# Moving a projection, two score products and a reciprocal within an attention tile of a fused four-layer kernel

## The reference

```python
x = x + tanh(g_xattn[0]) * attention(layernorm(x), mask, ctx, Wq, Wk, Wv, Wo, gate)
x = x + tanh(g_ffn[0])   * top1_experts(layernorm(x), wg, W, b)
x = x + tanh(g_xattn[1]) * wkv(w, u, k=layernorm(x), v=ctx)
x = x + tanh(g_ffn[1])   * top2_experts(layernorm(x), w_gate, w1, w2, w3)
```

## Time and profile before

| | us |
|---|---|
| median of 3 runs | 498.11 |
| range of the runs | 497.46 to 499.47 |
| the profiled execution, its own time | 498.84 |
| its span in the trace | 496.7 |
| PE busy in the span | 461.7 (93%) |
| DVE busy | 376.7 (76%) |
| ACT busy | 259.4 (52%) |
| POOL busy | 175.8 (35%) |

### The profile page before, as it was taken

One profiled execution on the slowest core, in us unless ns is written; L12 is line 12 of the kernel. 1 busy time (PEld: TensorE's weight loads), 2 busy tenths in 40 slices (PEclk: granted clock), 3 DMA queues, 4 the chain that ended last, 5 costly groups with the idle time before them and its releaser, 6 DMA issues. The chain is left out here.

```text
span 496.7 us, 10389 instructions
## 1 busy us (share of the span) xinstructions
PE 461.7 (93%) x3123; PEld 347.1 (70%) x3124; DVE 376.7 (76%) x1007; ACT 259.4 (52%) x562; POOL 175.8 (35%) x228
## 2 busy tenths in 40 slices
PE   4979999998999999999989999999999999999993
PEld 2648677686686776866857755566777878788782
DVE  5876788998988889989877889767867566566540
ACT  2765384572752845737513343326565766657641
POOL 4134213225124232241131160315446557555522
PEclk9999999999999999999999899999999999999998
DMA  7951304004022040040130689648566767768511
GB/s 217 287 107 29 63 1 86 18 13 86 22 44 53 21 84 15 12 84 16 38 69 21 255 341 366 193 116 298 170 205 215 251 183 245 223 197 252 162 22 21
DMA packets 24769, 63.37 MB, mean 128 GB/s; under 512 B 5176, under 2 KB 15296, under 8 KB 21792
## 3 DMA queue, kind: packets, MB, share of 16 engines
q1 hardware_dynamic: 19456, 56.38, 37.2%
q0 software_dynamic: 4416, 6.03, 6.6%
q10 hardware_dynamic: 864, 0.54, 0.3%
HBM read 48.79 MB, written 5.24 MB: 109 GB/s over the span
## 5 line engine op out<-in xcount | busy, mean ns | idle before, releaser
L2021 PE MATMUL bank_o<-w,hT 128*128 (+1 forms) x276 | 68.3, 389 | 1.9 <-issue 1.0
L1406 DVE TENSOR_TENSOR wl<-lw,wh 128x1024 fp32r<-128x1024 f32 (+1 forms) x54 | 60.9, 1129 | 1.1 <-ACT wh L639 1.1
L2021 PEld LDWEIGHTS bank_o<-w,hT 128*128 128x128 f32 (+1 forms) x276 | 48.8, 189 | 16.2 <-issue 11.4
L639 ACT ACTIVATE wh<-lw 128x1024 fp32r<-128x1024 f32 (+1 forms) x54 | 52.9, 981 | 1.8 <-DMA lw<-in_w 1.8
L1091 DVE TENSOR_REDUCE mx<-bank_s 128x8 f32<-128x512 f32 x64 | 42.6, 687 | 11.0 <-PE bank_s L1756 10.7
L498 POOL TENSOR_SCALAR rstd<-mv 128x1 f32<-128x1 f32 x32 | 9.3, 289 | 111.5 <-DVE mv L1011 111.5
L1754 PE MATMUL bank_s<-Kh,Qx 128*128 128x128 f32 x256 | 40.9, 282 | 1.5 <-DVE mx L1091 1.0
L593 POOL DMA_INDIRECT out_x<-ys,idx_out x18 | 29.0, 1609 | 35.3 <-ACT ys L911 33.6
L1754 PEld LDWEIGHTS bank_s<-Kh,Qx 128*128 128x128 f32 x256 | 35.8, 190 | 6.2 <-DVE mx L1091 3.3
L1399 DVE TENSOR_TENSOR hh<-sg,bank_s 128x256 f32<-128x256 f32 x46 | 19.0, 418 | 27.2 <-ACT sg L900 25.3
L1811 PEld LDWEIGHTS bank_o<-Vx,Pt 128*64 128x64 f32 x1024 | 32.5, 138 | 10.0 <-issue 5.5
(11 more groups left out here) (352 smaller groups left out, 1147.4 us busy)
## 6 DMA issues: line engine op xcount, KB each, us to landing
lw<-in_w SPq DMA_DIRECT2D x18, 1408.0 KB, 6.3
Q<-Qx SPq DMA_DIRECT2D x16, 512.0 KB
up<-in_w SPq DMA_DIRECT2D x5, 1408.0 KB, 7.4
w<-in_w SPq DMA_DIRECT2D x4, 1536.0 KB, 12.6
Pt<-in_WT SPq DMA_DIRECT2D x1, 1024.0 KB, 11.6
CT<-in_ctxT SPq DMA_DIRECT2D x1, 896.0 KB, 9.1
X<-in_x SPq DMA_DIRECT2D x1, 768.0 KB, 8.0
out_x<-X SPq DMA_DIRECT2D x6, 128.0 KB, 1.7
```

Of the source, the lines that this page charges most:

```text
L639: return act.activation(dst, src, ACT.Copy, scale=scale)
L1406: dve.tensor_tensor(wl[par][:, :, at:at + k], lw[par][:, :, at:at + k], wh[par][:, :, at:at + k].bitcast(F32), ALU.subtract).then_inc(w_lo, 1)
L2021: ins = pe.matmul(bo[:, 0:HID], hT[0:k, i, :], w2[0:k, bass.ts(e, 1), i, :].rearrange("p o n -> p (o n)"), start=(i == 0), stop=(i == IT - 1))
```

## The change

Three lists are reordered, and TensorE gets two more products per pass, for t = 1 to 6. ScalarE: the evacuation of the second batch moves from behind the first half of `spread` to the place between the gate's exponential and `evac_comb`. VectorE: `wkv_inverse` (t = 2 to 6) moves ahead of the gate's chain, behind `shift_low`. TensorE: `project_kv(t + 1, 1)` moves ahead of `turn_h2`; two constant products are added between `turn_maxima` and `gate_logits`; the `scores` halves of attend 0 and 1 move to the place between `turn_q` and `turn_comb`; what stays at their old places is `low_and_shift`.

```diff
@@ -836,10 +836,10 @@
                 high_h2(t - 1)
                 evac_v(t + 1, 1 - par, 0)
                 gate(t - 1)
+                evac_v(t + 1, 1 - par, 1)
                 evac_comb(t - 1)
                 evac_qT(t + 1)
                 spread(t + 1, 1 - par, range(HG // 2))
-                evac_v(t + 1, 1 - par, 1)
                 exps(t, 0)
                 spread(t + 1, 1 - par, range(HG // 2, HG))
                 exps(t, 1)
@@ -1513,9 +1513,9 @@
                 rope_q(t + 1)
                 sum_q(t + 1)
                 shift_low(t)
-                gate(u)
                 if prev2:
                     wkv_inverse(w)
+                gate(u)
                 low_q(t + 1)
                 if prev2:
                     wkv_out(w)
@@ -2099,20 +2099,23 @@
                 output(t - 1)
                 row_scores(t, par, range(6, 8))
                 project_kv(t + 1, 0)
+                project_kv(t + 1, 1)
                 turn_h2(t - 1)
                 turn_maxima(t)
+                constant_products(bo, 2)
                 gate_logits(t - 1)
                 turn_q(t + 1)
-                project_kv(t + 1, 1)
+                scores(t, par, 0, 0, True, True)
+                scores(t, par, 0, 1, True, True)
                 turn_comb(t - 1)
                 experts0(t - 1, 0)
                 experts0(t - 1, 1)
                 if prev2:
                     turn_y(t - 2)
-                attend(t, par, 0, True, True)
+                low_and_shift(t, par, 0, 0)
                 experts0(t - 1, 2)
                 experts0(t - 1, 3)
-                attend(t, par, 1, True, True)
+                low_and_shift(t, par, 0, 1)
                 bias0(t - 1)
                 attend(t, par, 2, True, True)
                 second_half(t, par, prev2, nxt2)
```

## The result

The changed kernel takes 521.29 us (median of 6 runs, 520.03 to 523.88) against 498.46 us before (6 runs): ratio 1.0458, 95% interval 1.0421 to 1.0495. That is 22.8 us slower. I had forecast 513.7 with a range of 505 to 521, so the direction is right and the time lies just outside the range. The profiled execution took 520.14 us with a span of 518.0 us. That is 21.3 us above the profiled execution of the kernel before (span 496.7), a little less than the medians differ by.

A forecast was written before the change was run, and what follows sets the result against it. The prediction saw three engines taking turns without slack around the gate, delaying VectorE's low_q and mixes. Tiles 2 to 6 (13.6) plus tile 1 (2.0) gave +15.6 on the profiled 498.84: 514.4, so median 513.7, range 505 to 521.

The forecast's parts named there:

- Steps 1 to 7: From early projection to first mix in tile 4: norm turned 1.14 later, standstill about 2.4, turn_comb 3.2 later, low_q 2.7 later.
- Step 8: Behind turn_comb: VectorE has no pause between the mixes, so the tile moves by its 2.7, not TensorE's 2.3.
- the sum: Whole kernel: tiles 2 to 6 give 5 x 2.7 = 13.6, tile 1 gives 2.0, together +15.6.
- TensorE's count: Per tile: turn_comb's delay of 3.2 less 0.9 of moved products, 2.3 later.
- rival (a): Per tile, VectorE has room and TensorE's accounting holds: 12.6 more, 510.7; at the far end 507.0; chance 0.25.
- Rival (b): TensorE's clock falls in the new standstill: 1.4 for one fall, 8.6 in all six tiles, so 522; chance 0.08.
- The sign that the prediction itself had named: Tiles of the changed kernel: the forecast is wrong if the clock there is below 1.00.
- a single stretch of a single execution: Tile 0 of the kernel before: TensorE waits 1.19, 1.86 busy of 4 us, clock 1.00; cited against the clock's fall.
- the cheap half of (b): Lower part of the clock fall's cost, taken into the range of 505 to 521; the dear half lay beyond.
- (c): At turn_comb: if it came by about 160.3, the delay would be covered; 2.5 less, 495.6; chance 0.05.
- (d): At the reciprocal and turned norm: sums late, or norm late anyway, and moves cancel within 2 us; chance 0.05.

The follow-up runs named there:

- e2: Changed kernel with eight constant products added behind the scores of batch 0, in TensorE's standstill: 514.01 us.
- e7: Changed kernel with four constant products in TensorE's standstill, behind the scores of batch 0: 513.78 us.
- e1: Changed kernel with the reciprocal moved back behind the gate's chain: 508.12 us.
- e4: Changed kernel with ScalarE's second evacuation ahead of the gate's exponential instead of behind it: 510.41 us.
- e6: Kernel before with only the second projection ahead of the turned norm and the two constant products: 507.38 us.
- e10: Changed kernel with the reciprocal of tiles 2 to 6 cut from 256 columns to one, leaving out the division there: 508.09 us.
- e3: Kernel before with only the reciprocal moved ahead of the gate's chain: 503.68 us.
- e5: Kernel before with only the scores of group 0, batch 0 moved ahead of turn_comb: 499.03 us.
- e8: Kernel before with the reciprocal of tiles 2 to 6 on GpSimd as a power of -1, and wkv_out, the third residual and turn_y placed later: 689.67 us.
- e9: Kernel before with the reciprocal of tiles 2 to 6 cut from 256 columns to one, leaving out the division there: 497.82 us.

## Why the prediction was wrong in size

**Steps 1 to 7 held.** The norm's turning 3.44 behind the first projection was exact, the shift's low part 0.96 later than before (3.55 to 4.51 behind the first projection; forecast 1.0), turn_comb at 9.02 (forecast 162.63 - 153.51 = 9.12), low_q later by 2.6 to 2.8 (forecast 2.7), the standstill 0.4 + 2.0 (forecast 2.4 in one piece: the scores of batch 0 already waited 0.38 for their Vx, which was called fine).

**Step 8 held for tiles 2 to 6.** With the clock at 1.00 (e2, e7) they grow by 2.7 each. Five give 13.4; the sum had 13.6. TensorE's count would have given 3.1 less 0.9, or 2.2. In e1, e2, e4, e6 and e10, too, the period without falls grows by what low_q is later, within 0.1. e3 is the exception, 1.13 for 0.85: there TensorE's turn_comb is 1.3 later and nothing was moved ahead to make up for it.

**Tile 1 was over-sized.** It grew by 1.2, not 2.0, though turn_comb and low_q came 2.1 later, as reckoned. There VectorE's mixes wait for TensorE before and after, so TensorE's own count holds, 2.1 less the 0.9 of products moved ahead. The same count gives 2.0 for e2 and 1.4 for e4, where tile 1 grew by 2.0 and 1.5. That is rival (a), and I had used step 8 in a tile without the reciprocal, wkv_out and the third residual that fill VectorE. The second mix of tile 1, before and after:

```profile
63.22 1.00 DVE L1146 SCALAR_TENSOR_TENSOR X<-bank_t,comb,X 128x256 f32<-128x256 f32 x2 [0.31 <-PE bank_t L1871]
```

```profile
64.39 1.00 DVE L1146 SCALAR_TENSOR_TENSOR X<-bank_t,comb,X 128x256 f32<-128x256 f32 x2 [0.32 <-PE bank_t L1871]
```

**The step that failed is the clock, a term the sum had at zero.** Rival (b) was given 0.08 and one fall 1.4 us. It came in every one of tiles 2 to 6 and costs 1.6 each: 5 x (37.57 - 35.98) = 8.0. By terms: 1.2 + 13.4 + 8.0 = 22.6, against 22.8 between the medians. (In the profiled pair the tiles give the same 22.5; what lies ahead of tile 1 and in tile 7 was 1.3 us shorter, which leaves the 21.3 of the spans.) The forecast's terms with five falls at its own price give 15.6 + 7 = 22.6 too, but that is luck: 0.8 too much for tile 1 and 0.2 for the others cancel 1.0 too little for the falls. The sign that the prediction itself had named, a clock below 1.00 in these tiles, is what came. The error was in the weighing: the forecast itself said that TensorE would stand still for 2.4 us, and leaned on a single stretch of a single execution with a clock of 1.00, whose wait was 1.19. The range was then cut at "the cheap half of (b)", although (b), if it comes, comes in all tiles. The rule of the Trainium skill that stood beside the rival (TensorE: Matmul & The Clock Gate, "A second HAM failure mode: psum-queue depth-cycling") says that short idles between groups of products can make the clock swing between its levels. The trace of the changed kernel agrees: 0.55 behind five standstills out of five. It agrees in kind only; what makes these idles here is an order of waits, not the cycling through PSUM banks which that page describes.

**The shares.** The projection ahead, with the two constant products, costs 1.14 a tile by itself (e6). With the scores and the evacuation ahead as well it is 1.45 (e1). The reciprocal adds 1.2 (e2 less e1), and 1.6 more through the clock, since only with it does TensorE's wait for Vx grow from 0.8 to 2.0. Of the parts that ran alone, only the scores of batch 0 are free (e5); the scores of batch 1 and the evacuation did not run alone, and their shares are not shown. Rivals (c) and (d) are out: turn_comb came 3.1 later, not within 0.9, and the reciprocal began 0.20 behind the shift's low part, with no wait for its sums.

## What to carry to other kernels

Ahead of a chain that goes round three engines, work that is "only moved" is not free, even on an engine that is busy 96% of the time; follow the chain link by link through each in-order queue, since that gave 2.7 for 2.7. When such a count says that TensorE will stand still for some 2 us, put the lower clock into the sum at once, for every repetition of the place: it fell five times in five. For 0.7 to 1.6 us, where it fell now and then, put it in as a chance, and do not let one execution's clock of 1.00 speak against it. Independent products in the gap are a cheap test, and a cheap remedy: four of them brought back 7.5 of 22.8 us. They do not bring back what the order itself costs.

## What the runs showed of the hardware that I had not expected

- The clock falls or holds for the same wait from one execution to the next. In the profiled runs it fell after a wait of 0.73 to 0.81 in one tile of 13 (tiles 1 to 6 of e1 and e10, tile 1 of the changed kernel), after 1.15 in none of five (e3), after 1.19 to 1.21 in tile 0 in two of twelve (e4, e7), after 1.56 in one of six (e6). After 0.3 to 0.4 and then 2.0 it fell five times in five. What decides it for the same wait is not shown.
- GpSimd's power takes 41.1 us on 128 x 256 (e8), against 0.57 to 0.64 us on 128 x 1. Spread over its columns that is 0.16 us each.
- A reciprocal of 1.7 us on VectorE is worth 0.2 us a tile behind the gate's chain (e9) and 2.8 ahead of it (e10).
